# Sum layer of a four-layer graph network: tiles in groups of 20 instead of 11, one-hots of eight tiles by one comparison

## The reference, cut to what matters

```python
h = jnp.maximum(_layernorm(x, axis=-1), 0.0)
x = x + jax.ops.segment_sum(h[src], dst, num_segments=3125)
```

## Time and profile before

| what | value |
|---|---|
| median of 3 runs | 3623.91 us (3616.06 to 3626.77) |
| the profiled execution's own time | 3605.4 us |
| its span, first to last instruction | 3603.6 us |
| mean granted TensorE clock over the span | 0.807 |
| gathers of the sum layer | from 1644.6 us to 2000.8 us |
| residual addition behind the sum layer | starts at 2017.61 us |
| busy over the whole span: PE, DVE, ACT, POOL | 72%, 71%, 16%, 64% |

### The profile page before, as it was taken

How to read it: one execution, slowest core, us unless ns; L and a number is a source line. 1 busy time by engine, 2 the same in 40 slices (tenths; PEclk the granted TensorE clock), 3 DMA queues, 4 the chain that set the end, 5 groups by cost and what they waited for, 6 DMA issues and landing times. The chain is left out here.

```text
span 3603.6 us, 57390 instructions
## 1 busy us (share of the span) xinstructions
PE 2602.2 (72%) x19362; PEld 1786.6 (50%) x19499; DVE 2548.7 (71%) x7445; ACT 576.6 (16%) x1352; POOL 2289.0 (64%) x2253
## 2 busy tenths in 40 slices
PE   0600000899998999996999799999999967777761
PEld 0300000777775777774666466666666544333331
DVE  9400000988983988878999777777777659999987
ACT  0100000000001000000111122222222213333320
POOL 2777776877770777775777455555555357777740
PEclk9655555778885788887999799999999969888875
DMA  6300001111113111111111100000000011111120
GB/s 97 104 8 8 8 8 58 31 22 23 24 15 100 25 23 23 23 13 29 29 29 29 13 10 10 10 10 11 10 11 10 6 24 27 27 27 27 27 18 5
DMA packets 125024, 91.60 MB, mean 25 GB/s; under 512 B 59542, under 2 KB 110678, under 8 KB 124118
## 3 DMA queue, kind: packets, MB, share of 16 engines
q0 software_dynamic: 70912, 41.10, 9.2%
q1 hardware_dynamic: 53846, 46.89, 5.7%
HBM read 60.42 MB, written 27.41 MB: 24 GB/s over the span
## 5 line engine op out<-in xcount | busy, mean ns | idle before, releaser
L732 POOL DMA_INDIRECT rel_rows<-message_table,message_indices x640 | 716.3, 1119 | 279.2 <-issue 194.4
L1287 POOL DMA_INDIRECT flow_x<-node_table,flow_index x440 | 443.1, 1007 | 401.2 <-DVE flow_index L1302 292.2
L1425 PE MATMUL flow_acc_bwd<-flow_onehot_j,flow_by_q 128*128 128x309 bf16 (+1 forms) x2503 | 552.2, 334 | 8.9 <-issue 0.2
L795 DVE TENSOR_SCALAR rel_source_onehot<-rel_sources,node_numbers 128x384 bf16<-128x384 f16 x2000 | 508.1, 315 | 62.6 <-PE p_rel_picked L870 61.4
L393 POOL DMA_INDIRECT sorted_edges<-stage,sorted_row x416 | 404.8, 973 | 191.9 <-issue 126.5
L1653 POOL DMA_INDIRECT att_kv_rows<-kv_table,att_index x440 | 424.0, 964 | 140.6 <-issue 129.8
L870 PE MATMUL p_rel_picked<-rel_source_onehot,rel_h_parts 128*96 128x384 bf16 x2000 | 429.4, 384 | 0.4 <-DVE rel_source_onehot L795 0.4
L870 PEld LDWEIGHTS p_rel_picked<-rel_source_onehot,rel_h_parts 128*96 128x96 bf16 x2000 | 297.0, 149 | 122.1 <-issue 0.7
L664 PE MATMUL p_rel_terms<-ident,source_centred 128*128 128x128 f32 (+1 forms) x4 | 1.1, 436 | 455.8 <-DVE source_centred L650 455.8
L1036 POOL DMA_INDIRECT sum_rows<-node_table,src_indices x280 | 271.2, 968 | 85.2 <-issue 85.2
L761 DVE COPY p_rel_lanes<-iota 128x128 f32<-128x128 f32 x2 | 0.6, 294 | 440.1 <-PEq L388 437.5
(11 more groups left out here) (286 smaller groups left out, 4979.9 us busy)
## 6 DMA issues: line engine op xcount, KB each, us to landing
message_table<-message_rows SPq DMA_DIRECT2D x50, 320.0 KB, 2.1
rel_rows<-message_table,message_indices POOLq DMA_INDIRECT x640, 2.7
rel_sources<-source_rows SPq DMA_DIRECT2D x80, 96.0 KB
flow_x<-node_table,flow_index POOLq DMA_INDIRECT x440, 2.4
att_kv_rows<-kv_table,att_index POOLq DMA_INDIRECT x440, 2.5
sorted_edges<-stage,sorted_row POOLq DMA_INDIRECT x416, 2.1
sum_sources<-source_rows SPq DMA_DIRECT2D x40, 128.0 KB, 3.2
sum_rows<-node_table,src_indices POOLq DMA_INDIRECT x280, 2.4
```

The source lines that it names most:

```text
L732: pool.indirect_dma_start(out=rows[b][:, t, :], out_offset=None, in_=d["messages"], in_offset=bass.IndirectOffsetOnAxis(ap=s["idx_msg"][:, ...
L795: last = dve.tensor_scalar(which[g % 2][:, c, :], srcs[b][:], s["node"][:, c:c + 1], None, ALU.is_equal)
L1287: pool.indirect_dma_start(out=X[b][:, t, 0:F], out_offset=None, in_=d["nodes"], in_offset=bass.IndirectOffsetOnAxis(ap=ibuf[b][:, t:t + 1] ...
L1425: last = pe.matmul(accB[:, lo:hi], S[b][:, t, k, :], J[b][:, t, lo:hi], start=False, stop=True, skip_group_check=True)
```

## The change

- Groups of 20 tiles, 12 gathered and 8 picked: 22 groups, 264 gathered and 176 picked tiles. Three buffers instead of four for rows, destination one-hots and source numbers.
- One comparison covers all eight picked tiles, 1024 columns. The one-hots go through a ring of six pieces of five chunks each (a fifth of a group); a semaphore counts the pieces made (`piece_ready`), another the pieces used (`piece_used`).
- A product over 1024 columns is two matmuls of 512 columns, into two banks: 50 matmuls a group.
- TensorE's order within a group: pick pieces 0 and 1 of g, load the column registers of g-1, first six gathered tiles of g-1, turn g-1, pieces 2 and 3 of g, last six gathered tiles of g-1, piece 4 of g, picked tiles of g-1.
- The parts of h are made in `x_centred` and `x_squared`; the copy of h at L1057 goes.
- SyncE loads 256 KB of source numbers a group and waits for `piece_ready`.

The diff, cut to its core:

```diff
-    G, PT, bufs = 11, 4, 4
-    rounds = T // G // bufs
+    G, PT, bufs = 20, 8, 3
+    groups = T // G
+    PIECE, SLOTS = NB // FIFTHS, 6
+    half = PT // 2 * P
-        hpart = sb(st, "sum_h_parts", [P, 3, NB * F])
...
-            which = [sb(st2, f"sum_source_onehot{b}", [P, NB, PT * P], BF16) for b in range(2)]
+            which = [sb(st2, f"sum_source_onehot{b}", [P, PIECE, PT * P], BF16) for b in range(SLOTS)]
...
-            pp = [ps(st2, f"p_sum_picked{b}", [P, BANK]) for b in range(2)]
+            pp = [ps(st2, f"p_sum_picked{b}", [P, 2 * BANK]) for b in range(2)]
...
-                            sp.wait_ge(which_ready, g - bufs + 1)
+                            sp.wait_ge(piece_ready, (g - bufs + 1) * FIFTHS)
...
-                    v.done(dve.tensor_copy(hpart[:, 0], s["h"][:]))
-                    v.done(split_parts(dve, v, hpart[:]))
-                    for j in range(3):
-                        last = dve.tensor_copy(hs[:, :, j, :], top(hpart[:])[:, j].rearrange("p (b f) -> p b f", f=F))
+                    v.done(dve.tensor_tensor(s["xc"][:], s["h"][:], top(s["h"][:]), ALU.subtract))
+                    v.done(dve.tensor_tensor(s["sq"][:], s["xc"][:], top(s["xc"][:]), ALU.subtract))
+                    for j, n in enumerate(("h", "xc", "sq")):
+                        last = dve.tensor_copy(hs[:, :, j, :], top(s[n][:]).rearrange("p (b f) -> p b f", f=F))
...
-                    def sources(g, lo, hi):
-                        for c in range(lo, hi):
-                            last = dve.tensor_scalar(which[g % 2][:, c, :], srcs[g % bufs][:], node[:, c:c + 1], None,
-                                                     ALU.is_equal)
-                        return last
+                    def sources(g, n):
+                        piece = g * FIFTHS + n
+                        if n == 0:
+                            dve.wait_ge(src_in[g % bufs], g // bufs * 16 + 16)
+                        if piece >= SLOTS:
+                            dve.wait_ge(piece_used, piece - SLOTS + 1)
+                        for c in range(PIECE):
+                            last = dve.tensor_scalar(which[piece % SLOTS][:, c, :], srcs[g % bufs][:],
+                                                     node[:, n * PIECE + c:n * PIECE + c + 1], None, ALU.is_equal)
+                        last.then_inc(piece_ready, 1)
...
                 @block.scalar
                 def _(act):
-                        act.wait_ge(pick_done, g + 1)
+                        act.wait_ge(piece_used, (g + 1) * FIFTHS)
...
+                    def columns(g):
+                        pe.load(regs[g % 2], s["dcol"][0:1, 0, g * G:(g + 1) * G])
...
+                    def pick(g, n):
+                        piece = g * FIFTHS + n
+                        pe.wait_ge(piece_ready, piece + 1)
+                        if n == 0 and g >= 2:
+                            pe.wait_ge(pick_taken, g - 1)
+                        for c in range(PIECE):
+                            for x in range(2):
+                                last = pe.matmul(pp[g % 2][0:3 * F, x * half:(x + 1) * half],
+                                                 hs[:, n * PIECE + c].rearrange("p k f -> p (k f)"),
+                                                 which[piece % SLOTS][:, c, x * half:(x + 1) * half],
+                                                 start=(n + c == 0), stop=(n * PIECE + c == NB - 1))
+                        last.then_inc(piece_used, 1)
+
+                    def gathered_rows(g, lo, hi):
                         b = g % bufs
                         pe.wait_ge(hot_ready, g + 1)
                         pe.wait_ge(gathered[b], g // bufs * (16 * GT) + 16 * GT)
-                        for t in range(GT):
+                        for t in range(lo, hi):
                             last = add(g, t, hot[b][:, t, :], [rows[b][:, t, :]])
-                        last.then_inc(rows_used, 1)
+                        if hi == GT:
+                            last.then_inc(rows_used, 1)
...
-                    pick(0)
-                    for g in range(groups):
-                        if g + 1 < groups:
-                            pick(g + 1)
-                        turn(g)
+                    for g in range(groups + 1):
+                        if g < groups:
+                            pick(g, 0)
+                            pick(g, 1)
+                        if g >= 1:
+                            columns(g - 1)
+                            gathered_rows(g - 1, 0, GT // 2)
+                            turn(g - 1)
+                        if g < groups:
+                            pick(g, 2)
+                            pick(g, 3)
+                        if g >= 1:
+                            gathered_rows(g - 1, GT // 2, GT)
+                        if g < groups:
+                            pick(g, 4)
                         if g >= 1:
                             picked_rows(g - 1)
-                        if g == groups - 1:
-                            picked_rows(g)
-                        gathered_rows(g)
```

More of the change, by code:

```diff
@@ L996, in sum_layer @@
 def sum_layer(nc, a, s, d, sb, ps, sem, more):
-    G, PT, bufs = 11, 4, 4
-    rounds = T // G // bufs
-    assert rounds * bufs * G == T
+    G, PT, bufs = 20, 8, 3
+    groups = T // G
+    assert groups * G == T
     GT = G - PT
+    PIECE, SLOTS = NB // FIFTHS, 6
+    half = PT // 2 * P
     with ExitStack() as st:
         zeros = sb(st, "sum_zeros", [1, BANK])
-        hpart = sb(st, "sum_h_parts", [P, 3, NB * F])
         hs = sb(st, "sum_h_stack", [P, NB, 3, F], BF16)
@@ L1023, in sum_layer @@
             src_in = [sem(st2, f"sum_sources_in{b}") for b in range(bufs)]
-            hot_ready, which_ready, rows_used, used, pick_done, pick_taken, turn_done, turn_taken = (
-                sem(st2, f"sum_{n}") for n in ("onehot_ready", "source_onehot_ready", "rows_used", "used", "pick_done",
-                                               "pick_taken", "turn_done", "turn_taken"))
+            hot_ready, piece_ready, piece_used, rows_used, used, pick_taken, turn_done, turn_taken = (
+                sem(st2, f"sum_{n}") for n in ("onehot_ready", "source_onehot_ready", "source_onehot_used", "rows_used",
+                                               "used", "pick_taken", "turn_done", "turn_taken"))
             with nc.Block() as block:
@@ L1030, in _ @@
                     more["pool"](pool)
-                    for g in range(rounds * bufs):
+                    for g in range(groups):
                         b = g % bufs
@@ L1066, in onehots @@
                                                  ALU.is_equal)
-                    def sources(g, lo, hi):
-                        for c in range(lo, hi):
-                            last = dve.tensor_scalar(which[g % 2][:, c, :], srcs[g % bufs][:], node[:, c:c + 1], None,
-                                                     ALU.is_equal)
-                        return last
-                    for g in range(rounds * bufs):
+                    def sources(g, n):
[8 more added lines that the diff above has]
+                        last.then_inc(piece_ready, 1)
+                    for g in range(groups):
                         b = g % bufs
-                        dve.wait_ge(src_in[b], g // bufs * 16 + 16)
-                        if g >= 2:
-                            dve.wait_ge(pick_done, g - 1)
                         for n in range(FIFTHS):
-                            last = sources(g, n * NB // FIFTHS, (n + 1) * NB // FIFTHS)
+                            sources(g, n)
                             if n == 0 and g >= bufs:
@@ L1087, in _ @@
                                 onehots(hotb[b][:], g * G + GT, PT).then_inc(hot_ready, 1)
-                        last.then_inc(which_ready, 1)
                     more["dve"](dve)
@@ L1092, in _ @@
                 def _(act):
-                    for g in range(rounds * bufs):
-                        act.wait_ge(pick_done, g + 1)
+                    for g in range(groups):
+                        act.wait_ge(piece_used, (g + 1) * FIFTHS)
                         if g >= 2:
                             act.wait_ge(turn_done, g - 1)
-                        act.copy(turned[g % 2][:], pp[g % 2][0:3 * F, 0:PT * P]).then_inc(pick_taken, 1)
+                        act.copy(turned[g % 2][:], pp[g % 2][0:3 * F, :]).then_inc(pick_taken, 1)
                         act.wait_ge(turn_done, g + 1)
@@ L1106, in _ @@
                     clear_acc(pe, s, zeros, [acc[:, 0:BANK], acc[:, BANK:2 * BANK]])
-                    regs = [[pe.alloc_register(f"sum_col{i}{t}") for t in range(G)] for i in range(3)]
-                    unused = [pe.alloc_register(f"sum_unused{i}") for i in range(3)]
+                    regs = [[pe.alloc_register(f"sum_col{i}{t}") for t in range(G)] for i in range(2)]
+                    def columns(g):
```

(3 more changed lines are left out.)

1 line of the change is left out of this document (removed).

## The result

Over 19 runs each the changed kernel takes 3635.63 us and the kernel before 3611.85 us (medians). The ratio is 1.0058, with a 95% interval of 1.0042 to 1.0075: about 21 us more. The forecast was 3600.5 us and faster; the time lies inside the printed range, but on the other side of no change. The price is the first rival's; its mechanism, gathers that starve in the chains, turns out to be a good third of it.

What follows compares the result with a forecast made beforehand. VectorE was taken to set the sum layer's pace, GpSimd nearly level. After the change, GpSimd at 1.298 us a gather puts the residual addition at 1994.2 instead of 2017.61: 3623.9 - 23.4 = 3600.5 us, range 3587 to 3650.

Steps and rivals of the forecast that it cites:

- the first rival: Sum layer: gathers starve until a chain of comparisons ends; 1.485 us a gather, +25.4 us, 3649 us; chance 0.30.
- the mean delay of a gather: GpSimd in the sum layer: waiting for 1024-column comparisons adds 0.053 us to an undisturbed gather of 0.944 us.
- A mean over 1.05 us: Sum layer: the forecast was declared wrong if gathers averaged over 1.05 us; 0.98 to 1.02 would show it right.
- The formula: Gather's mean wait: (streaming time)^2 / (2 x step), by the share of time in comparisons, times 0.73; 0.053 us for 1024 columns.
- the 512-column row: Sum layer before: the formula gave a mean wait of 0.033 us among 512-column comparisons, 0.024 measured; hence the factor 0.73.
- The tail: End of the sum layer: last gather lands after 2.4 us, TensorE's remaining work 4.5, residual addition 0.3 later.
- The break-even of 1.388 us a gather: Sum layer: at 1.388 us between gathers, a gather of 1.09 us, the change alters nothing.
- the 2.42 us gather: Relational layer: a gather from 1207.65 to 1210.07, read as waiting for the end of a chain of five comparisons.
- The Trainium skill's rule of full blocking: VectorE in two-port mode and GpSimd exclude each other for whole instructions; taken as: no gather gets in within a chain.
- The clock rival: TensorE in the sum layer: waits for gathers halve its clock, 16.2 us a group; only -9 us, 3615 us; chance 0.12.
- the slow comparison: VectorE in the sum layer: the wide comparison takes 0.57 us, 17.6 us a group; +26 us, 3650 us; chance 0.05.

Runs made afterwards that it cites:

- narrow: The changed kernel with each 1024-column comparison made as two of 512; one run, 405.8 us from first gather to residual addition (changed kernel 397.0).
- long_chain: The kernel before with a group's four one-hot instructions behind all 25 comparisons; one run, 388.2 us from first gather to residual addition (before 373.0).
- alternate: The changed kernel with destination one-hots made one tile at a time after each of a piece's first four comparisons; ratio to the kernel before 0.9985.
- pairs: The changed kernel with a two-tile one-hot instruction after every second or third comparison; one run, 374.3 us from first gather to residual addition (changed kernel 397.0).

## Why the prediction was wrong

**The step that failed** is the mean delay of a gather, 0.053 us; it measured 0.214 (1.158 less 0.944). At 1.463 us a gather (from the third at 1645.04 to the last at 2026.82) instead of 1.298, 261 gathers take 43.1 us more than forecast. That is nearly all of the 47.4 us between the forecast stretch (373.0 - 23.4) and the measured one. A mean over 1.05 us was the prediction's own sign against itself. The formula had two premises, and neither holds:

- *"It asks at any moment."* It does not. A gather takes 0.94 us and the next asks 0.30 us later, so gathers and comparisons run in a fixed rhythm, and a bad phase comes back (in narrow every 35.5 us). Half of the gathers lie in the group of 0.1 to 0.4 us, with a mean delay of 33.0 / 133 = 0.25 us, near 0.293, the most that the formula lets one comparison cost; 54 of them are over that. If a gather can be held at two moments, as the ends point to, it has two chances to be late, and the formula gave it one.
- *"It is served after the comparison in progress."* Mostly, but 18 gathers of the changed kernel, nine of narrow and two of long_chain were not.

That the formula met the 512-column row (0.033 against 0.024) was no test of it: that loop ran in one good rhythm, and a single rhythm is one draw. The trace of before held a row on which it fails. For the relational layer's 384 columns it gives at most 0.110^2 / (2 x 0.24) = 0.025 us (0.110 us is 384 x 0.286 ns, and (1.27 - 0.30) / 4 = 0.24 us the step), where the mean delay is 0.175. The prediction read that row as the rival's and not as a test of its own formula.

**The tail** was put at 2.4 + 4.5 + 0.3 = 7.2 us and measured 12.0; this is the other 4.8 us. 2.7 us of it are rows that came late: the adds began 5.1 us after the last gather, not 2.4. Why, no run shows; alternate and pairs have the same tail of 12.0 us. The other 2.1 us are TensorE's remaining work at half clock (0.50 granted in the stretch from 2031 to 2038), after 9.7 us without work. The prediction had 7 us for this case and took 4.5.

**Right** were the steps around it. 25 comparisons and the one-hots leave VectorE waiting (median comparison 474 ns, 480 forecast; steps in a chain (2.06 - 0.47) / 4 = 0.40). An undisturbed group of TensorE takes 14.3 us (14.5 forecast; the timeline row of picks at 1940.19 comes back at 1954.48). GpSimd becomes the bound. No picks wait for comparisons in the steady state. The break-even of 1.388 us a gather holds up with the longer tail taken in (4.8 / 261 = 0.02 less): pairs, with (1999.29 - 1640.26) / 261 = 1.376 us a gather, has a stretch of 374.3 us beside 373.0 before.

**The rivals.** The first was priced at r = 1.485 and +25.4 us; measured 1.463 and +24.0 us for the stretch, +21 for the kernel. Its price was right, its mechanism only in part, so some luck is in the price: starved gathers make 20.6 of the 56.6 us of delay, shorter waits of 0.1 to 0.4 us make 33.0. Its example, the 2.42 us gather, was read too simply: it began in the chain before the one named there, and a one-hot ran from 1208.39 to 1208.93 in its middle without ending it. The wait for one chain does not account for it. I gave the rival 0.30 because the sum layer's own gathers looked clean; long_chain and narrow show that they only stood in a good phase. The Trainium skill's rule of full blocking (page "SBUF — State Buffer", section "Who interferes with whom"), taken as the prediction took it, fits the starved gathers alone; most of the others that ran beside comparisons ended while a chain was still running. The clock rival did not happen in the steady state (0.91 granted in the window above), nor did the slow comparison.

The number itself owes something to where it was counted from. The forecast of 3600.5 us stands on a median of 3623.9 for the kernel before, over three runs; over 19 it is 3611.85. The same saving counted from there would have been 3588.5 us.

What stays open is what decides, at the end of one comparison in a chain, whether the gather or the next comparison goes first. The phase alone does not. Two gathers of the changed kernel start at the same point of a chain of five, 0.20 us into it, to within a few thousandths of a microsecond; one starves and one gets in:

```profile
1677.54 2.05 DVE L1076 TENSOR_SCALAR sum_source_onehot<-sum_sources,node_numbers 128x1024 bf16<-128x1024 f16 x5
1677.73 1.97 POOL L1037 DMA_INDIRECT sum_rows<-node_table,src_indices  x1 [0.30 <-issue]
...
1805.06 2.05 DVE L1076 TENSOR_SCALAR sum_source_onehot<-sum_sources,node_numbers 128x1024 bf16<-128x1024 f16 x5
1805.26 1.18 POOL L1037 DMA_INDIRECT sum_rows<-node_table,src_indices  x1 [0.30 <-issue]
```

I have not found a rule for it, and no run here was made to find one.

## What to carry to other kernels

When an engine is sped up and another runs beside it at nearly the same level, ask what the faster form takes from the neighbour; here the comparison that lowers VectorE's step per column from 0.51 to 0.39 ns (0.262 us for 512, 0.40 for 1024) also held gathers up for longer at a time: by up to 0.09 us in the sum layer before, mostly by 0.1 to 0.4 us after. A gather's duration read from one loop is a property of that loop's rhythm, so bound it by the worst loop in the trace, and let that end have its weight. Where fast comparisons and gathers must run together, put an instruction of another form between every two comparisons: the same one-hots in smaller pieces, one behind every comparison, were worth 39 us here.

## What the runs showed of the hardware that I had not expected

- A gather can be shut out through 25 back-to-back comparisons of 512 columns (6.64 us), while nearly all others of the same run lie in such chains without delay.
- A gather of 0.944 us seems to be held at one of two moments, about 0.13 and 0.82 us after its start: in the changed kernel 150 of the 155 late ones end 0.81 or 0.12 us after the end of a comparison.
- The wait can be moved from one engine to the other: 1.158 us a gather and 484 ns a comparison in chains, 0.948 us and 532 ns when spaced.
- Comparisons made by TENSOR_TENSOR with one operand in PSUM held no gather up, long as they are: 0.94 us beside comparisons of 1.2 us.
